# A selective-scan and window-attention kernel: two of sixteen states turned by TensorE and multiplied by ScalarE

## What is computed

```python
xz = xn @ in_proj_w.T                     # xn: group norm, then layer norm
xc = silu(conv1d(xb) + conv_b)            # 4 taps, one filter a channel
dt = softplus(x_dbl[:, :24] @ dt_w.T + dt_b)
h  = exp(dt * A) * h + (dt * x) * B       # over tokens, for 16 states n
y  = sum_n(h * C) + xc * D
out = (y * silu(z)) @ out_proj_w.T        # added to x
```

## Time and profile before

| | |
|---|---|
| median of 3 runs | 6866.09 us (6865.48 to 6866.52) |
| the profiled execution's own time | 6863.25 us |
| its span | 6861.5 us |
| TensorE's mean granted clock | 0.939 |
| scan stage, first to last tile | 186.2 to 5534.4 us of the span |
| busiest engines over the span | DVE 89%, PE 87% |

### The profile page before, as it was taken

One profiled execution on the slowest core, in us unless ns is written; L12 is line 12 of the kernel. 1 busy time (PEld: TensorE's weight loads), 2 busy tenths in 40 slices (PEclk: granted clock), 3 DMA queues, 4 the chain that ended last, 5 costly groups with the idle time before them and its releaser, 6 DMA issues. The chain is left out here.

```text
span 6861.5 us, 99209 instructions
## 1 busy us (share of the span) xinstructions
PE 5990.6 (87%) x32906; PEld 3756.6 (55%) x32906; DVE 6138.1 (89%) x7731; ACT 4716.2 (69%) x8759; POOL 5351.3 (78%) x4333
## 2 busy tenths in 40 slices
PE   4888888888888888888888888888888879999998
PEld 2455555555555555555555555555555547777776
DVE  4899999999999999999999999999999956666665
ACT  1777777777777777777777777777777743333332
POOL 0999999999999999999999999999999930101010
PEclk9999999999999999999999999999999989999999
DMA  4322222222222222222222222222222232222222
GB/s 186 114 112 111 112 109 112 102 101 101 100 102 101 101 101 103 104 101 102 100 101 102 100 101 104 104 101 102 101 101 101 108 125 71 78 79 77 81 73 68
DMA packets 177702, 694.99 MB, mean 101 GB/s; under 512 B 28332, under 2 KB 28556, under 8 KB 143140
## 3 DMA queue, kind: packets, MB, share of 16 engines
q1 hardware_dynamic: 177188, 688.65, 27.0%
HBM read 512.57 MB, written 157.09 MB: 98 GB/s over the span
## 5 line engine op out<-in xcount | busy, mean ns | idle before, releaser
L774 POOL TENSOR_TENSOR dbx<-u,bb 128x512 f32<-128x512 f32 x3072 | 3829.4, 1280 | 29.9 <-DVE p_da L673 14.8
L673 DVE TENSOR_TENSOR_SCAN p_da<-p_da,state_v,dbx 128x512 f32<-128x512 f32 x2112 | 2620.8, 1273 | 54.6 <-ACT p_da L548 54.6
L548 ACT ACTIVATE p_da<-dt,neg_a 128x512 f32<-128x512 f32 x3076 | 2076.1, 687 | 83.6 <-DVE h L680 8.2
L898 PEld LDWEIGHTS p_yt<-ident,hc_v 128*128 128x128 f32 x8448 | 1108.8, 151 | 1137.1 <-issue 843.0
L898 PE MATMUL p_yt<-ident,hc_v 128*128 128x128 f32 x8448 | 1381.5, 293 | 162.9 <-DVE hc_v L689 162.4
L689 DVE TENSOR_TENSOR hc_v<-cc,p_da 128x512 f32<-128x512 f32 x2112 | 1391.4, 666 | 0.0
L783 POOL TENSOR_TENSOR hc_g<-h,cc 128x512 f32<-128x512 f32 x960 | 1227.6, 1279 | 108.4 <-DVE h L680 108.3
L680 DVE TENSOR_TENSOR_SCAN h<-p_da,state_g,dbx 128x512 f32<-128x512 f32 x960 | 1218.1, 1269 | 103.8 <-ACT p_da L548 103.5
L839 PE MATMUL p_g<-xs,win 128*128 128x512 f32 x2376 | 1208.6, 603 | 74.7 <-ACT zt L500 36.3
L554 ACT ACTIVATE state_v<-p_da 128x1 f32<-128x1 f32 x2112 | 351.0, 166 | 914.2 <-DVE hc_v L689 901.8
L1321 POOL TENSOR_TENSOR x_low<-axn,x_upper 128x512 fp32r<-128x512 f32 x96 | 127.3, 1355 | 1045.9 <-DVE x_upper L1273 1045.9
(11 more groups left out here) (153 smaller groups left out, 7397.5 us busy)
## 6 DMA issues: line engine op xcount, KB each, us to landing
bb<-bc_spill SPq DMA_DIRECT2D x132, 1024.0 KB, 10.4
cc<-bc_spill SPq DMA_DIRECT2D x132, 1024.0 KB, 10.2
xc_spill<-xc SPq DMA_DIRECT2D x99, 512.0 KB, 2.6
z_spill<-zt SPq DMA_DIRECT2D x99, 512.0 KB, 3.9
xj<-xc_spill SPq DMA_DIRECT2D x193, 256.0 KB, 4.1
zj<-z_spill SPq DMA_DIRECT2D x192, 256.0 KB, 2.7
xs<-in_x SPq DMA_DIRECT2D x34, 768.0 KB, 5.7
xc<-in_x SPq DMA_DIRECT2D x33, 768.0 KB, 11.9
```

The source lines that it names most:

```text
L548: nc.scalar.activation(p_da[n % RD][:], dt[:, d % 2, :], ACT.Exp, scale=neg_a[:, d, n:n + 1])\
L673: nc.vector.tensor_tensor_scan(psum, psum, dbx[:, n % RB, :], state_v[:, d, k:k + 1], ALU.mult, ALU.add).then_inc(s_scan, 1)
L774: nc.gpsimd.tensor_tensor(dbx[:, n % RB, :], u[:, d % 2, :], bb[:, n, :], ALU.mult)\
L898: last = nc.tensor.matmul(p_yt[d % 2][:, b * P:(b + 1) * P], product[:, b * P:(b + 1) * P], ident[:], start=False, stop=n == NS - 1, is_tr ...
```

## The change

States 7 and 11 (BY_TURN) are multiplied with C neither by DVE nor by GpSimd. DVE scans them into h, which has now seven buffers, one for each state of BY_H. TensorE turns the state by four transpositions into the p_yt bank that `project_dt` and `softplus` have just used (`turn_state`, steps 9 and 12). There tokens lie on partitions, so C of a state is one number a partition: ScalarE multiplies each quarter with a column of ct as its scale and writes it to hct (`times_ct`, steps 11 and 14). `turn_back` of the next tile turns yt_s and then both hct back into the same sum. C itself is turned once a chunk (`turn_c`, `copy_ct`).

GpSimd keeps five states, 14 in place of 12, and its product of state 14 is made in the next tile's step 1. DVE keeps nine. hc_v has three buffers, not five. cc holds 14 rows, not 16. The steps of most of the work beside the scan move, `copy_y` from 3 to 2, `softplus` from 6 to 7, `skip` from 8 to 10, `dt_x` from 15 to 13, and the copies and silus as listed. `add_skip` waits for both `times_ct` of the tile before.

```diff
-BY_POOL = (0, 3, 6, 9, 12)
-BY_DVE = tuple(n for n in range(NS) if n not in BY_POOL)
-NDV, NPL = len(BY_DVE), len(BY_POOL)
-RB, RH, RD = 4, 5, 4
-RV, RG = 5, 3
-LAG, LAG_V, LAG_G = 3, 2, 3
+BY_POOL = (0, 3, 6, 9, 14)
+BY_TURN = (7, 11)
+BY_DVE = tuple(n for n in range(NS) if n not in BY_POOL + BY_TURN)
+BY_H = tuple(sorted(BY_POOL + BY_TURN))
+BY_C = tuple(n for n in range(NS) if n not in BY_TURN)
+NDV, NPL, NTN, NHS = len(BY_DVE), len(BY_POOL), len(BY_TURN), len(BY_H)
+LAST_ADDED = max(BY_DVE + BY_POOL)
+
+RB, RH, RD = 4, NHS, 4
+RV, RG = 3, 3
+TURN_STATE_AT, TIMES_CT_AT, KEEP_AT = (9, 12), (11, 14), 14
+LAG, LAG_V, LAG_G = 3, 2, 2
-MEAN_AT, CENTRE_AT, SQUARE_AT = 2, (3, 7, 9), (7, 8, 9)
-VAR_AT, RSTD_AT, NORM_AT = 12, 11, (15, 16, 17)
-OUT_AT, OUT_SLOTS, RESIDUAL_AT = (9, 15, 19), (3, 1, 1), (14, 20, 23)
-IN_AT, IN_SLOTS = (20, 39, 57), (18, 18, 19)
-COPY_LATER, SILU_LATER = 2, (4, 2, 3)
-X_AT, COPY_X_AT, SCALE_AT = (80, 82, 83), 83, (87, 90, 92)
-
-COPY_Y_AT, TURN_AT, GATE_AT = 3, 4, 6
-DT_AT, SOFTPLUS_AT, SKIP_AT, DT_X_AT = 6, 6, 8, 15
+MEAN_AT, CENTRE_AT, SQUARE_AT = 2, (3, 8, 10), (2, 7, 8)
+VAR_AT, RSTD_AT, NORM_AT = 10, 11, (16, 17, 18)
+OUT_AT, OUT_SLOTS, RESIDUAL_AT = (6, 14, 19), (2, 2, 1), (12, 19, 25)
+IN_AT, IN_SLOTS = (22, 41, 59), (18, 18, 19)
+COPY_LATER, SILU_LATER = 1, (8, 2, 2)
+X_AT, COPY_X_AT, TURN_C_AT, COPY_CT_AT, SCALE_AT = (78, 81, 82), 84, 85, 95, (89, 90, 93)
+
+COPY_Y_AT, TURN_AT, GATE_AT = 2, 4, 6
+DT_AT, SOFTPLUS_AT, SKIP_AT, DT_X_AT = 6, 7, 10, 13
...
-                src = bc_d[q, NS + 4 * k:NS + 4 * k + 4, :].rearrange("(o n) t -> o n t", o=1).to_broadcast([P, 4, CH])
-                sp.dma_start(cc[:, 4 * k:4 * k + 4, :], src).then_inc(s_cl[k], 16)
+                these = [n for n in BY_C if n // 4 == k]
+                at, count = BY_C.index(these[0]), len(these)
+                src = bc_d[q, NS + these[0]:NS + these[0] + count, :].rearrange("(o n) t -> o n t", o=1)
+                sp.dma_start(cc[:, at:at + count, :], src.to_broadcast([P, count, CH])).then_inc(s_cl[k], 16)
...
+            def copy_ct(q):
+                act.wait_ge(s_ctm, q + 1)
+                if q > 1:
+                    act.wait_ge(s_ht, (q - 1) * (ND * NTN) + NTN)
+                turned = p_g[1][:, 0:NT * 64].rearrange("p (b c) -> p b c", c=64)
+                nc.scalar.activation(ct[:, q % 2], turned[:, :, 32 + NS:64], ACT.Copy).then_inc(s_ct, 1)
+
+            def times_ct(i, d, n):
+                m, k = i * ND + d, BY_TURN.index(n)
+                act.wait_ge(s_tm, m * NTN + k + 1)
+                if k == 0:
+                    act.wait_ge(s_yb, m + 1 + C_ONE)
+                if d == 0 and k == 0:
+                    act.wait_ge(s_ct, i + 1)
+                for b in range(NT):
+                    last = nc.scalar.activation(hct[:, k, b, :], p_yt[(d + 1) % 2][:, b * P:(b + 1) * P], ACT.Copy,
+                                                scale=ct[:, i % 2, b, n:n + 1])
+                last.then_inc(s_ht, 1)
...
+                        if n in TIMES_CT_AT:
+                            times_ct(i, d, BY_TURN[TIMES_CT_AT.index(n)])
...
+                        if g == COPY_CT_AT:
+                            copy_ct(q)
...
-                    k = BY_POOL.index(n)
-                    dve.wait_ge(s_hcg, m * NPL + k + 1)
-                    dve.wait_ge(s_stg, m * (NPL // RH) + k // RH + C_ONE)
-                    nc.vector.tensor_tensor_scan(h[:, k % RH, :], psum, dbx[:, n % RB, :], state_g[:, d, k:k + 1],
+                    k = BY_H.index(n)
+                    if n in BY_POOL:
+                        dve.wait_ge(s_hcg, m * NPL + BY_POOL.index(n) + 1)
+                    elif m:
+                        dve.wait_ge(s_tm, (m - 1) * NTN + BY_TURN.index(n) + 1)
+                    dve.wait_ge(s_stg, m + C_ONE)
+                    nc.vector.tensor_tensor_scan(h[:, k, :], psum, dbx[:, n % RB, :], state_h[:, d, k:k + 1],
...
-            def keep_state(i, d, k):
-
-                n = BY_POOL[k * RH + RH - 1]
-                dve.wait_ge(s_scan, (i * ND + d) * NS + n + 1 + C_SCAN)
-                nc.vector.tensor_reduce(state_g[:, d, k * RH:(k + 1) * RH], h[:, :, CH - 1:CH], AX.X, ALU.max)\
-                    .then_inc(s_stg, 1)
+            def keep_states(i, d):
+
+                dve.wait_ge(s_scan, (i * ND + d) * NS + BY_H[-1] + 1 + C_SCAN)
+                nc.vector.tensor_reduce(state_h[:, d, :], h[:, :, CH - 1:CH], AX.X, ALU.max).then_inc(s_stg, 1)
...
+                        if n < LAG and i + d > 0 and n - LAG + NS in BY_POOL:
+                            times_c(*((i, d - 1) if d > 0 else (i - 1, ND - 1)), n - LAG + NS)
...
-                    pe.wait_ge(s_xd, i + 1)
+                    pe.wait_ge(s_ct, i + 1)
...
+                pe.wait_ge(s_ht, m * NTN + NTN)
...
                     last = nc.tensor.matmul(p_yt[(d + 1) % 2][:, b * P:(b + 1) * P], yt_s[:, b * P:(b + 1) * P],
+                                            ident[:], start=b == 0, stop=m == 0, is_transpose=True,
+                                            skip_group_check=True)
+                for k in range(NTN if m else 0):
+                    pe.wait_ge(s_ht, (m - 1) * NTN + k + 1 + NTN)
+                    for b in range(NT):
+                        last = nc.tensor.matmul(p_yt[(d + 1) % 2][:, b * P:(b + 1) * P], hct[:, k, b, :],
+                                                ident[:], start=False, stop=k == NTN - 1, is_transpose=True,
+                                                skip_group_check=True)
+                last.then_inc(s_yb, 1)
+
+            def turn_c(q):
+
+                pe.wait_ge(s_xd, q + 1)
+                for b in range(NT):
+                    last = nc.tensor.matmul(p_g[1][:, b * 64:(b + 1) * 64], xd[:, b * P:(b + 1) * P],
+                                            ident[0:64, 0:64], start=True, stop=True, is_transpose=True)
+                last.then_inc(s_ctm, 1)
+
+            def turn_state(i, d, n):
+
+                m, k = i * ND + d, BY_TURN.index(n)
+                pe.wait_ge(s_scan, m * NS + n + 1 + C_SCAN)
+                pe.wait_ge(s_dt, m + 2)
+                pe.wait_ge(s_ht, m * NTN + k + NTN)
+                for b in range(NT):
+                    last = nc.tensor.matmul(p_yt[(d + 1) % 2][:, b * P:(b + 1) * P], h[:, BY_H.index(n), b * P:(b + 1) * P],
                                             ident[:], start=True, stop=True, is_transpose=True)
-                last.then_inc(s_yb, 1)
+                last.then_inc(s_tm, 1)
...
+                        if g == TURN_C_AT:
+                            turn_c(q)
+                        if n in TURN_STATE_AT:
+                            turn_state(i, d, BY_TURN[TURN_STATE_AT.index(n)])
```

More of the change, by code:

```diff
@@ L260, in scan_layer @@
         bb = sb("bb", [P, NS, CH])
-        cc = sb("cc", [P, NS, CH])
+        cc = sb("cc", [P, len(BY_C), CH])
         dbx = sb("dbx", [P, RB, CH])
@@ L266, in scan_layer @@
         state_v = sb("state_v", [P, ND, NDV])
-        state_g = sb("state_g", [P, ND, NPL])
+        state_h = sb("state_h", [P, ND, NHS])
+        ct = sb("ct", [P, 2, NT, NS])
+        hct = sb("hct", [P, NTN, NT, P])
         yt_s = sb("yt_s", [P, CH])
@@ L290, in scan_layer @@
         s_stg = sem("state_kept_dve")
+        s_ctm = sem("c_turned_mm")
+        s_ct = sem("c_turned")
+        s_tm = sem("state_turned_mm")
+        s_ht = sem("state_turned")
         s_dbx = sem("dbx_done")
@@ L427, in body @@
                             v = i * (ND * NDV) + 5 * NDV + sum(n < 4 * k + 4 for n in BY_DVE) + C_HCV
-                            g = i * (ND * NPL) + 5 * NPL + sum(n < 4 * k + 4 for n in BY_POOL) + RH
+                            g = i * (ND * NPL) + 5 * NPL + sum(n < 4 * k + 4 for n in BY_POOL) + NPL
                             sp.wait_ge(s_hcv, v)
@@ L452, in _ @@
             act.sem_inc(s_stv, C_STV)
+            act.sem_inc(s_ht, NTN)
             act.preload_act_table_set(EXP_LN)
@@ L573, in _ @@
             copy_xd(0)
+            copy_ct(0)
             for j in range(NJ):
@@ L688, in times_c @@
                     dve.wait_ge(s_cl[n // 4], i * 16 + 16)
-                nc.vector.tensor_tensor(hc_v[:, (m * NDV + k) % RV, :], cc[:, n, :], p_da[n % RD][:], ALU.mult)\
+                nc.vector.tensor_tensor(hc_v[:, (m * NDV + k) % RV, :], cc[:, BY_C.index(n), :], p_da[n % RD][:], ALU.mult)\
                     .then_inc(s_hcv, 1)
-            def keep_state(i, d, k):
-                n = BY_POOL[k * RH + RH - 1]
-                dve.wait_ge(s_scan, (i * ND + d) * NS + n + 1 + C_SCAN)
-                nc.vector.tensor_reduce(state_g[:, d, k * RH:(k + 1) * RH], h[:, :, CH - 1:CH], AX.X, ALU.max)\
-                    .then_inc(s_stg, 1)
+            def keep_states(i, d):
+                dve.wait_ge(s_scan, (i * ND + d) * NS + BY_H[-1] + 1 + C_SCAN)
+                nc.vector.tensor_reduce(state_h[:, d, :], h[:, :, CH - 1:CH], AX.X, ALU.max).then_inc(s_stg, 1)
             for j in range(NJ):
```

(20 more changed lines are left out.)

## The result

| | before | changed kernel |
|---|---|---|
| median | 6866.31 us (4 runs) | 6817.8 us (6816.38 to 6822.56, 4 runs) |
| ratio | | 0.993, 95% interval 0.9915 to 0.9945 |
| profiled execution, its span | 6863.25, 6861.5 us | 6818.65, 6816.9 us |
| TensorE's mean granted clock | 0.939 | 0.949 |

The change saves 48.5 us, 0.7%. The forecast was 6776, 90 us; the time lies in the stated range (6735 to 6895) and just above the forecast's own (6735 to 6815).

A forecast was written before the change was run, and what follows sets the result against it. GpSimd's 163.0 us a chunk was taken as the floor, with DVE equally full. Of 4.1 us lost a chunk 1.3 would remain: 2.8 x 32 = 90 us less, so 6776 us; range 6735 to 6895, the forecast's own 6735 to 6815.

The forecast's parts named there:

- What bounds: Scan stage: DVE 98% and GpSimd 97% busy; GpSimd's 163.0 us a chunk is the floor, only its waiting can be gained.
- 227 us if DVE were alone: Scan stage: 7.1 us a chunk x 32 would go if DVE alone were the bound; the prediction says it isn't.
- ScalarE's instruction: Products of turned states: eight 128x128 activations a tile, 0.354 us each, one every 0.28; 2.2 us a tile, net +1.9.
- TensorE's sum and the chain: Transpositions add 0.9 to 1.7 us a tile; work queued through the one p_yt bank causes no DVE wait at full clock.
- Rival (3): Chain through the single p_yt bank makes decay(15) and add_skip late in every tile: slower, for example 6952 us; chance 0.22.
- What GpSimd still loses: GpSimd's waiting in tiles 0 and 1, partly recovered in tiles 2 to 5: 1.3 us a chunk lost, of 4.1 before.
- The sign that I named: Scan stage: if the forecast is right, GpSimd's waits for DVE fall from 123 us to about 40.
- The silus' block: ScalarE after the second silus group, before decay(2): 6.3 us against about 5 of p_da cover, costing about 1.2 us.
- The low clock: TensorE at half clock in tiles 5 and 0: up to 1.5 us in each, mostly swallowed by DVE's recovery.
- Tile 1: Tiles 0 and 1: DVE needs 56.9 us against GpSimd's 54.3, may trail by about 2.5; 0.1 to 0.5 us lost.
- rival (1): TensorE, busy throughout tile 1, holds it: only a partial gain, 6820 to 6845 us; with similar gains, chance 0.14.
- similar partial gains: Whole kernel: the band of 6815 to 6852 us, including the case that TensorE holds tile 1; chance 0.14.

The follow-up runs named there:

- Experiment 1: The changed kernel with the second group of silus at step 64 in place of 61: 6768.79 us, ratio 0.9855.
- experiment 6: The changed kernel without three DVE statistics instructions a chunk: 6773.85 us; in another run, without three of six matmuls of the third output projection: 6803.93 us.

## Why the prediction was right or wrong

**What bounds: right.** GpSimd holds the tiles at 27.0 to 27.2 us; the floor a chunk is 6 x 27.04 = 162.2 us (163.0 put; the 0.8 is the step of u). DVE gave up 202 us of busy time and 48 reached the end. The answer "227 us if DVE were alone" was rightly refused.

**ScalarE's instruction: right.** 0.354 us for 128 columns put, 0.360 measured; four end 1.14 us after the first starts and take 1.0 of the engine (2958.11 to 2959.10), 1.1 put. Its busy share is 4484.59 / 5299.80 = 85%, 87% put.

**TensorE's sum and the chain: right in the main.** ScalarE waits for a turned state 23.8 us in 192 tiles. TensorE waits for hct 114.2 + 87.4 us, 1.05 us a tile and so just over the 1 us that the prediction named as a sign of being wrong; it comes in two waits a chunk, and DVE's gate waits 4.8 us in all, where it waited 9.0. Rival (3) did not come up. hc_v's three buffers cost 26.7 us of DVE's waiting, mostly covered, and a fourth gave 8 us or nothing.

**The step that failed is "What GpSimd still loses".** I put 1.3 us a chunk, of 4.1 before; it is 165.7 - 162.2 = 3.5, so 0.7 us a chunk were recovered and not 2.8. The sign that I named, GpSimd's waits down to about 40 us, did not come: they are 96. Three terms were mis-sized:

- The silus' block. I counted 6.3 us against 5 of cover. The copy of the input projection that falls into it (0.83 us) was left out, and the cover was 3.9 us (2952.65 to 2956.55), since it ends where DVE has used its last p_da, not four states later. Stall 3.3 us, 3.8 in the chunks at the full clock, not 1.2. GpSimd's side covered 2.8 of the 3.8 (2.5 put), so tile 4 lost 1.0 us at the full clock. Experiment 1 takes it all back.
- The low clock. I priced it for tiles 5 and 0 and had it swallowed. Those tiles do take 27.06 and 27.03 us, but the delay shows one tile later: 0.8 us of tile 4 in 22 of 31 chunks (clock 0.94 over tile 3, which I took for full), 1.2 us of tile 1 in 14 of 31 (clock 0.71 to 0.75 over tile 0). That is 0.55 us a chunk each, 1.1 x 32 = 35 us in all. No run sets the clock alone: this price is read from chunks of the two kinds. The mean clock of the whole kernel rose even so, from 0.939 to 0.949, and doesn't show it.
- Tile 1. I put 0.1 to 0.5 us; it is 28.79 - 27.04 = 1.75. In the 14 chunks without that wait it is 1.0: DVE's sum, as the step says and experiment 6 shows. The sum was right and the room somewhat too large: 57 us against 54.1 is 2.9, of which 1.9 were covered and not 2.5. The rest is the low clock (0.55) and the first chunks of images (0.2, not in the prediction).

**Luck.** The time fell between the forecast and rival (1), in the band of "similar partial gains" that had 0.14, but half of its 48 us is not a recovered wait at all: 25 us are the 0.13 us a tile that u's move from step 15 to 13 gave GpSimd. The prediction names that move and takes it for neutral. Without it the change would have gained about 24 us, by this sum; no run moves u alone. Rival (1) is wrong as to tile 1's load (experiment 6) and half right in that a late TensorE lengthens tile 1.

## What to carry to other kernels

Of two engines that are both 97% busy, a relief of the one is worth at most what the other waits for it (123 us here, not DVE's 227), and it makes the next serial stretch of a third engine visible. On an engine that feeds a bound one in order, look at the longest run of instructions between two that are waited for, and put it against what the ring holds at that place: one constant that split such a run was worth as much as the change. Before work goes to an engine that will then be the bound, count its waits in full. Look at the single chunks and not only at their mean: the two levels here name a cause that no total shows. And on the engine that is the bound, an instruction that reads what the one before it made is worth moving apart.

## What was not expected of the hardware

GpSimd starts an instruction 1.23 us after the one before it, but 1.35 to 1.36 us after it where it waits for that one's result. That holds for u and the first times B in the kernel before, and in the two runs with turned states and u at step 15; with u at 13 it is 1.23 in the changed kernel and in the run with the moved steps alone. It is 0.13 us once a tile, 25 us over the stage, half of what the change gained. That the reading of the result is the reason fits all four kernels, but no run tests it by itself.
